# Layer 3's capped mixture: the slot-number products cut in two halves between the fallback's quarters, and every row fetch issued before the first result is sent

## The chip, the cores and the metric

The kernel runs on one core of one Trainium2 chip. The metric is the device time of one execution in microseconds. The whole decoder (four layers, twelve blocks) is one program; the change touches the last block alone, the mixture of experts of layer 3.

## The reference, cut to what matters

The block sees 2048 tokens of 128 features. A router gives each token two of eight experts. Each expert takes its first 320 tokens (CAP); a token that comes later overflows and gets a dense fallback network in place of what it had until then, and is not eligible for later experts.

```python
    def _L3_ffn_ref(x, Wr, W1, b1, W2, b2, fw1, fb1, fw2, fb2):
        D_MODEL, D_FF, N_EXPERTS, TOP_K = (128, 512, 8, 2)
        ...
        CAP = max(int(CAPACITY_FACTOR * (T * TOP_K / N_EXPERTS)), MIN_CAP)
        ...
        y_fb = jax.nn.gelu(xf @ fw1 + fb1, approximate=False) @ fw2 + fb2
        ...
        for e in range(N_EXPERTS):
            assign = experts == e
            w_e = jnp.where(assign, scores, 0.0).sum(-1)
            eligible = assign.any(-1) & ~fb_mask
            rank = jnp.cumsum(eligible.astype(jnp.int32)) - 1
            keep = eligible & (rank < CAP)
            overflow = eligible & ~keep
            fb_mask = fb_mask | overflow
            y = jnp.where(overflow[:, None], y_fb, y)
            idx = jnp.nonzero(keep, size=CAP, fill_value=0)[0]
            valid = jnp.arange(CAP) < keep.sum()
            h = jax.nn.gelu(xf[idx] @ W1[e] + b1[e], approximate=False)
            y_e = h @ W2[e] + b2[e]
            y = y.at[idx].add(y_e * (w_e[idx] * valid)[:, None])
        return y.reshape(Bx, Sx, D)
```

## The kernel before

Each stage of the program gives every engine its own list of instructions, written out by hand; an engine works its list in order, and the lists meet at counting semaphores (`wait_ge`, `then_inc`). There is no scheduler, so the order of the lines is the order on the engine. The stage here is `capped_mixture`. Nearly all its matmuls are recorded under one helper line, L468; the transposes of fetched rows are L3606.

**The dense part.** The fallback runs over all 2048 tokens in four jobs of 512 tokens. A job is an up product (`core.up_pe`, four matmuls of 128x512 into banks 0 to 3), a Gelu on ScalarE (L3421 in the profile, four per job), and a down product (`fallback_down_pe`). The down product of a job is a generator of four quarters. A quarter is four fp32 matmuls of 128x128 and one of a single row for the bias, into bank 6 or 7; ScalarE copies the finished bank away (`lower_act`, L3802).

**The ranks and the slots.** `cap_pe` and `cap_dve` walk the eight experts: VectorE forms who is eligible, two short bf16 products of 16 columns give the ranks, and a fallback quarter of job 0 or 1 stands after each such pair. `places_dve` and `spots_dve` then give each token's two slots: 21 blocks of 128 slots, kept in 32 groups, of which VectorE writes a one-hot `spot` table, four groups to an instruction (L3712, eight instructions), while GpSimd writes the `numbers` table in three instructions (L3831 to L3834). `numbers_pe` multiplies the two: 32 bf16 matmuls of 63 columns, all summed in bank 5, which tell which token fills each slot. `numbers_dve` turns that into two index lists, `source` (L3726) and `target` (L3727). `shares_dve` (seven VectorE instructions, L3731 to L3741) forms the weights with which results are added at the very end.

**The experts.** GpSimd fetches the rows of each expert's tokens out of a table in DRAM by indirect DMA (`fetch_pool`, L3839, one DMA for a block of up to 128 rows, 21 in all; experts 0 to 7 own 3, 2, 3, 2, 3, 2, 3, 3 of them). TensorE transposes them (`slots_pe`, L3606), VectorE copies the result into SBUF (L3761), the up product is four matmuls of 128x320 (`up_pe`), ScalarE's Gelu is L3822, the down product is twelve small matmuls (`down_pe`), and VectorE adds the bias (`result_dve`, L3769 and L3770). TensorE's list is, after the first two experts' slots and the first up product, in rounds: slots of expert n+2, up product of n+1, down product of n. GpSimd then sends each expert's result rows to DRAM, again by indirect DMA (`send_pool`, L3845, 21 in all; 2, 3, 2, 3, 2, 3, 3, 3). SyncE reads the results back (L3882), VectorE adds them to X (L3753), and X is stored (L3885).

**What sets the order around the change.** GpSimd's list is one queue. In it stand the fetches of experts 0 to 3, then a wait for the results of expert 0, its sends, the fetches of expert 4, the sends of expert 1 after a wait, the fetches of expert 5, and so on.

The names of tiles in the profile are those of memory areas: `scratch`, `w_keep` and `w_early` are arenas from which the stage takes its buffers. The fetched rows, their transposes and the results are in `w_keep`, and the weights of this stage in `w_early`.

Of the kernel before, what the change touches and what calls it, by code (L numbers as in the profile page):

```python
# [16 lines left out]
NT = B * HALVES  # L17
# [14 lines left out]
E8 = 8  # L32
# [47 lines left out]
class Signal:  # L80
# [21 lines left out]
    def at(self, *what):  # L102
        return self.of(self.k.stage, *what)
# [74 lines left out]
def tmp(k, cols, dt=F32):  # L178
    return carve(k, "scratch", cols, dt)
# [48 lines left out]
def join(k, e):  # L228

    for last in k.ended:  # L230
        e.wait_ge(*last)


def need(k, e, *packs):

    for name in packs:
        e.wait_ge(k.s.loaded[name].sem, 16)
# [153 lines left out]
def all_flat(k, e, tag):  # L391
    e.wait_ge(*flat(k, tag, 2))
    e.wait_ge(*flat(k, tag, 3))
# [6 lines left out]
def pre_norm_pe(k, pe):  # L400
    turn_pe(k, pe, "pre", lambda i: k.XN[:, i, :], lambda i: normed(k, "pre", i))
# [65 lines left out]
def mm(pe, out, lhsT, rhs, start=True, stop=True):  # L467
    return pe.matmul(out, lhsT, rhs, start=start, stop=stop, skip_group_check=True)  # L468
# [3047 lines left out]
def capped_mixture(k):  # L3516
# [7 lines left out]
    s, w = k.s, k.w  # L3524
# [8 lines left out]
    N2, SB = 2 * NT, SLOT_BLOCKS  # L3533
# [11 lines left out]
    numbers = tmp(k, N2 * 3 * SB, BF16).rearrange("p (i n b) -> p i n b", n=3, b=SB)  # L3545
# [27 lines left out]
    def fallback_down_pe(pe, job):  # L3573
        bank = k.bank[6 + job % 2]
        if job >= 2:
            pe.wait_ge(*s.lowered.at("fallback", job - 2))
        for c in (C - 2, C - 1):
            pe.wait_ge(*s.gated.at("h", job, c))
        for j in range(4):
            o = bank[:, j * P:(j + 1) * P]  # L3580
            for c in range(C):
                mm(pe, o, hidden[job % 2][:, c * BANK + j * P:c * BANK + (j + 1) * P], w["z_fw2"][:, c * D:(c + 1) * D], c == 0, False)
            m = mm(pe, o, w["ones"][0:1, :], w["z_fb2_bc"][0:1, :], False, True)
            if j == 3:
                m.then_inc(*s.summed.up("down", job))
            yield

    def numbers_pe(pe):

        pe.wait_ge(*s.vector.at("rank", E8 - 1))  # L3590
        pe.wait_ge(*s.pool.at("numbers"))
        for i in range(N2):
            if i % 4 == 0:
                pe.wait_ge(*s.cut.at("spot", i // 4))
            m = mm(pe, k.bank[5][:, 0:3 * SB], spot[:, i, :], numbers[:, i, :, :].rearrange("p n b -> p (n b)"), i == 0, i == N2 - 1)
        m.then_inc(*s.projected.up("numbers"))

    def slots_pe(pe, e):
        bank = k.bank[4 + e % 2]
# [27 lines left out]
    def pe(e):  # L3627
        join(k, e)
        need(k, e, "l3f")
        pre_norm_pe(k, e)  # L3630
        all_flat(k, e, "pre")
        core.logits_pe(e)
        core.up_pe(e, 0)
        core.up_pe(e, 1)
        e.wait_ge(*s.preset.at("after"))
        cap_pe(e)
        core.up_pe(e, 2)
        core.up_pe(e, 3)
        numbers_pe(e)
        for job in (2, 3):  # L3640
            for _ in fallback_down_pe(e, job):
                pass
        slots_pe(e, 0)
        slots_pe(e, 1)
        up_pe(e, 0)
        for n in range(E8):
            if n + 2 < E8:
                slots_pe(e, n + 2)
            if n + 1 < E8:
                up_pe(e, n + 1)  # L3650
            down_pe(e, n)
# [48 lines left out]
    def spots_dve(dve):  # L3700

        up, at = lambda n: s.vector.up("spot", n), lambda n: s.vector.at("spot", n)
        dve.wait_ge(*s.vector.at("place", "where"))
        dve.tensor_tensor(reached, where.unsqueeze(2).to_broadcast([P, N2, SB + 1]), starts.unsqueeze(1).to_broadcast([P, N2, SB + 1]),
                          ALU.is_ge).then_inc(*up("reached"))
        dve.wait_ge(*at("reached"))
        dve.tensor_reduce(block_of, reached[:, :, 1:SB + 1], AXX, ALU.add).then_inc(*up("block"))
        dve.wait_ge(*at("block"))
        dve.scalar_tensor_tensor(out=within, in0=block_of, scalar=-float(P), in1=where, op0=ALU.mult, op1=ALU.add).then_inc(*up("within"))
        dve.wait_ge(*at("within"))  # L3710
        for i in range(0, N2, 4):
            dve.tensor_tensor(spot[:, i:i + 4, :], w["steps"][:, 0:P].unsqueeze(1).to_broadcast([P, 4, P]),  # L3712
                              within[:, i:i + 4].unsqueeze(2).to_broadcast([P, 4, P]), ALU.is_equal).then_inc(*s.cut.up("spot", i // 4))

    def numbers_dve(dve):

        up, at = lambda n: s.vector.up("number", n), lambda n: s.vector.at("number", n)
        bank = k.bank[5]
        dve.wait_ge(*s.projected.at("numbers"))
        dve.tensor_scalar(free, bank[:, 2 * SB:3 * SB], -float(OUTSIDE), float(OUTSIDE), ALU.mult, ALU.add).then_inc(*up("free"))  # L3720
        dve.tensor_scalar(later, bank[:, 0:SB], float(NT), -float(T), ALU.is_ge, ALU.mult).then_inc(*up("later"))
        dve.tensor_scalar(number, bank[:, 0:SB], float(P), None, ALU.mult).then_inc(*up("tile"))
        dve.wait_ge(*at("tile"))
        dve.tensor_tensor(number, number, bank[:, SB:2 * SB], ALU.add).then_inc(*up("number"))
        dve.wait_ge(*at("number"))
        dve.tensor_tensor(source, number, later, ALU.add).then_inc(*s.formed.up("source"))  # L3726
        dve.tensor_tensor(target, number, free, ALU.add).then_inc(*s.formed.up("target"))  # L3727

    def shares_dve(dve):
        wgt = core.e3(core.wgt)  # L3730
        dve.tensor_tensor(wgt, wgt, every(live), ALU.mult).then_inc(*s.formed.up("routed"))  # L3731
        dve.wait_ge(*s.formed.at("routed"))
        for n in range(2):
            up, at = lambda x: s.vector.up("share", n, x), lambda x: s.vector.at("share", n, x)
            if n:
                dve.wait_ge(*s.vector.at("share", 0, "sum"))
            dve.tensor_tensor(same, slot, every(place[n]), ALU.is_equal).then_inc(*up("same"))
            dve.wait_ge(*at("same"))
            dve.tensor_tensor(same, same, wgt, ALU.mult).then_inc(*up("own"))
            dve.wait_ge(*at("own"))  # L3740
            dve.tensor_reduce(share[n], same, AXX, ALU.add).then_inc(*up("sum"))  # L3741
# [31 lines left out]
    def dve(e):  # L3773
        join(k, e)
        need(k, e, "l3f")
        pre_norm_dve(k, e)
        for _ in core.route_dve(e, "weights"):
            pass
        e.wait_ge(*s.formed.at("weights"))
        cap_dve(e)  # L3780
        places_dve(e)
        spots_dve(e)
        shares_dve(e)
        numbers_dve(e)
        turned_dve_(e, 0)
        turned_dve_(e, 1)
        for n in range(E8):
            if n + 2 < E8:
                turned_dve_(e, n + 2)
            result_dve(e, n)  # L3790
            if 1 <= n <= QUARTERS:
                fallback_dve(e, n - 1)
        e.wait_ge(*s.vector.at("share", 1, "sum"))
        for n in range(2):
            for q in range(QUARTERS):
                result_sums_dve(e, n, q)
# [39 lines left out]
    def fetch_pool(pool, e):  # L3836
        blocks = fetched_blocks(e)
        for block, n in blocks:
            pool.indirect_dma_start(rows[0:n, block, :], None, row_store, bass.IndirectOffsetOnAxis(ap=source[0:n, block:block + 1], axis=0),  # L3839
                                    bounds_check=T - 1, oob_is_err=False).then_inc(*s.slots_in[e].up(*(("rows",) if block == blocks[-1][0] else ("row", block))))  # L3840
# [7 lines left out]
    def pool(e):  # L3848
        join(k, e)
        e.memset(empty, 0.0).then_inc(*s.preset.up("empty"))  # L3850
        e.tensor_copy(after, w["after"]).then_inc(*s.preset.up("after"))
        for n in range(E8):
            e.memset(first_slot[:, n:n + 1], float(first_slot_of(n) - 1))
        for n in range(SB + 1):
            m = e.memset(starts[:, n:n + 1], float(n * P))
        m.then_inc(*s.pool.up("constants"))
        numbers_pool(e)
        e.wait_ge(*s.rows_out.at("rows"))
        e.wait_ge(*s.formed.at("source"))
        for n in range(4):  # L3860
            fetch_pool(e, n)
        e.wait_ge(*s.emptied.at("results"))
        e.wait_ge(*s.formed.at("target"))
        for n in range(E8):
            send_pool(e, n)
            if n + 4 < E8:
                fetch_pool(e, n + 4)

# [423 lines left out]
```

## Time and profile before

| what | us |
|---|---|
| median of 3 runs | 2503.71 (2494.99 to 2503.94) |
| the profiled execution's own time | 2502.37 |
| its span | 2500.6 |
| the capped mixture, from its first transposes to the end | 2358.1 to 2500.6 |
| TensorE's last matmul begins its group | 2475.53, 5.96 long |

The span is what the profiler saw from the first to the last instruction; the run's own time is 1.77 us longer. Times in rows count from the span's start. "Idle before" in a row's brackets is the time for which that engine did nothing ahead of the group, and the name behind the arrow is what ended it. PEclk is the granted clock of TensorE: 1.00 is 2.4 GHz, 0.50 is 1.2 GHz.

### The profile page before, as it was taken

The numbers are of one execution on the slowest core, as the hardware profiler recorded it, in microseconds if no ns is written. First come the engines' busy times: TensorE is split into PE (matmuls) and PEld (weight loads), VectorE is DVE, ScalarE is ACT, GpSimd is POOL, SyncE is SP. The second block draws the span as 40 slices with busy tenths as digits, with TensorE's granted clock in tenths as the row PEclk, the third lists the DMA queues.
The fourth block names the chain that finished last, engine by engine and source line by source line (L and its number), as shares of the span: only waits on it lengthen the run. The fifth ranks groups of instructions, "written<-read, shape, count | busy, mean of one in ns | idle before, by whom it ended". The sixth has DMA issues, their size and how long they took to land.

```text
span 2500.6 us, 40089 instructions
## 1 busy us (share of the span) xinstructions
PE 2000.8 (80%) x14320; PEld 1350.3 (54%) x14320; DVE 1543.0 (62%) x3580; ACT 1302.8 (52%) x2673; POOL 480.7 (19%) x539
## 2 busy tenths in 40 slices
PE   6999765878999999937764087999999897668795
PEld 4666552436777777613352064565666576434474
DVE  6777685756666566357656925666666457468533
ACT  4666543666777777416654125666666212336521
POOL 2112003103333223241003531000100001211024
PEclk9999986989999999859996598999999899779877
DMA  4000004310000000023201000000000100233102
GB/s 176 1 1 1 1 1 89 85 33 16 1 1 1 1 1 1 1 59 84 45 1 69 0 2 8 1 1 1 1 1 1 46 6 1 99 90 85 52 13 79
DMA packets 78631, 72.35 MB, mean 29 GB/s; under 512 B 8115, under 2 KB 71652, under 8 KB 77410
## 3 DMA queue, kind: packets, MB, share of 16 engines
q1 hardware_dynamic: 77089, 67.29, 9.5%
q0 software_dynamic: 1344, 2.49, 0.4%
q8 instruction: 117, 1.92, 0.3%
q14 instruction: 81, 0.66, 0.1%
HBM read 54.91 MB, written 14.97 MB: 28 GB/s over the span
## 4 chain that ended last, share of the span: by engine, by line
PE 50%; DVE 22%; SPq 9%; issue 7%; ACT 7%; DMA 4%; POOL 1%; DVEq 0%; ACTq 0%; POOLq 0%
PE bank L468 42%; SPq L1408 9%; DMA scratch<-parts 2%; DVE w_keep L1921 1%; PE bank L652 1%; PE bank L2868 1%; PE bank L368 1%; DVE stats L245 1%; PE bank L692 1%; ACT w_early L3109 1%; DVE w_early L2532 1%; DVE scratch L3007 1%; DVE scratch L720 1%; DMA parts<-scratch 1%; DVE XN L3042 1%
## 5 line engine op out<-in xcount | busy, mean ns | idle before, releaser
L468 PE MATMUL bank<-scratch 64*128 64x256 bf16 (+5 forms) x3696 | 397.1, 321 | 127.3 <-DMA scratch<-parts 88.2
L468 PEld LDWEIGHTS bank<-scratch 64*128 64x128 bf16 (+3 forms) x3696 | 222.3, 123 | 274.0 <-issue 80.8
L1225 DVE TENSOR_REDUCE scratch<-bank 128x2 f32<-128x512 f32 x384 | 245.8, 686 | 132.1 <-PE bank L468 129.3
L468 PE MATMUL bank<-w_keep,scratch 128*128 128x128 f32 (+4 forms) x1760 | 247.0, 333 | 35.3 <-ACT scratch L805 20.8
L1311 ACT ACTIVATE w_keep<-bank 128x512 f32<-128x512 f32 x384 | 210.2, 596 | 98.9 <-PE bank L468 93.5
L468 PE MATMUL bank<-XNT,w_keep 128*128 128x256 f32 (+4 forms) x800 | 238.3, 437 | 9.3 <-POOL w_keep L2169 4.6
L468 PEld LDWEIGHTS bank<-w_keep,scratch 128*128 128x128 f32 (+3 forms) x1760 | 184.3, 186 | 97.0 <-issue 46.6
L3109 ACT ACTIVATE w_early<-bank,scratch 128x256 f32<-128x256 f32 x256 | 123.5, 563 | 131.2 <-DVE scratch L3011 131.2
L468 PEld LDWEIGHTS bank<-XNT,w_keep 128*128 128x128 f32 x800 | 149.7, 197 | 62.7 <-issue 29.4
L468 PE MATMUL bank<-w_early,scratch 64*128 64x256 f32 (+3 forms) x1152 | 170.5, 354 | 11.1 <-ACT w_early L3109 8.5
L468 PEld LDWEIGHTS bank<-w_early,scratch 64*128 64x128 f32 (+3 forms) x1152 | 125.2, 192 | 66.3 <-issue 41.2
L468 PE MATMUL bank<-w_keep 128*32 128x256 f32 (+1 forms) x1792 | 136.0, 371 | 8.1 <-ACT w_keep L1311 7.3
L805 ACT ACTIVATE scratch<-bank,scratch 128x256 f32<-128x256 f32 x256 | 100.3, 474 | 77.2 <-DVE scratch L720 77.2
L468 PE MATMUL bank<-scratch,w_early 128*128 128x256 f32 (+2 forms) x416 | 126.0, 448 | 9.9 <-DVE scratch L2527 3.3
L3007 DVE TENSOR_REDUCE scratch<-bank 128x2 f32<-128x512 f32 x128 | 87.9, 686 | 71.4 <-PE bank L468 71.4
L468 PE MATMUL bank<-XNT,w_early 128*128 128x256 f32 (+1 forms) x384 | 119.2, 441 | 4.5 <-ACT XNT L383 1.6
L368 PE MATMUL bank<-w_keep,XN 128*128 128x128 f32 x192 | 47.3, 422 | 84.3 <-DVE XN L318 81.5
L720 DVE TENSOR_REDUCE scratch<-bank 128x2 f32<-128x512 f32 x128 | 82.3, 684 | 50.9 <-PE bank L468 50.8
L468 PEld LDWEIGHTS bank<-w_keep 128*32 128x32 f32 (+1 forms) x1792 | 75.0, 122 | 53.9 <-issue 34.0
L468 PEld LDWEIGHTS bank<-scratch,w_early 128*128 128x128 f32 x416 | 73.4, 203 | 50.1 <-issue 30.0
L1921 DVE SCALAR_TENSOR_TENSOR w_keep<-w_keep,w_early 128x256 f32<-128x256 f32 x192 | 96.5, 551 | 0.1
L468 PE MATMUL bank<-scratch,SEL 64*128 64x512 bf16 x384 | 77.1, 398 | 22.1 <-ACT scratch L1336 22.1
(449 smaller groups left out, 3740.7 us busy)
## 6 DMA issues: line engine op xcount, KB each, us to landing
scratch<-parts SPq DMA_DIRECT2D x768, 32.0 KB
parts<-scratch SPq DMA_DIRECT2D x24, 384.0 KB, 3.2
w_early<-pack_l3f SPq DMA_DIRECT2D x1, 5206.0 KB, 16.0
w_keep<-pack_l2f SPq DMA_DIRECT2D x1, 2124.0 KB, 12.8
w_early<-pack_mamba SPq DMA_DIRECT2D x1, 2120.0 KB, 19.0
w_keep<-pack_l2x SPq DMA_DIRECT2D x1, 2049.0 KB, 7.9
w_keep<-taps SPq DMA_DIRECT2D x4, 512.0 KB, 5.4
w_early<-wave_kernels SPq DMA_DIRECT2D x1, 2048.0 KB
```

Of the source, the lines that this page charges most:

```text
L245: dve.bn_stats(k.stats[:, i, :], src[:, i, :]).then_inc(*k.s.stats.up(tag, i))
L368: t = pe.transpose(k.bank[q][:, j * P:(j + 1) * P], src(i), k.w["ident"])
L468: return pe.matmul(out, lhsT, rhs, start=start, stop=stop, skip_group_check=True)
L652: m = pe.transpose(self.k.bank[3 + o][:, c * S + t * P:c * S + (t + 1) * P], self.expo[g % 4][:, t * S + c * P:t * S + (c + 1) * P], self. ...
L720: dve.tensor_reduce(self.neg[g % 4], self.scores(g)[:, :].rearrange("p (t s) -> p t s", s=S), AXX, ALU.max, negate=True).then_inc(*s.maxed ...
L805: a = act.activation(self.expo[g % 4][:, t * S:(t + 1) * S], self.scores(g)[:, t * S:(t + 1) * S], ACT.Exp, bias=self.neg[g % 4][:, t:t + 1])
L1225: dve.tensor_reduce(neg[:, :, h], self.k.bank[5 - g % 2][:, :].rearrange("p (t s) -> p t s", s=S), AXX, ALU.max, negate=True).then_inc(*s. ...
L1311: act.activation(self.expo[g % 8], k.bank[g % 4][:, :], ACT.Exp, scale=HD ** -0.5).then_inc(*s.weighed.up("e", g))
L1408: sp.dma_start(view[row:row + HD, n, :, :], src).then_inc(*s.loaded_stack(b % 3).up(*((b,) if last else (b, n, o, j))))
L1921: o = dve.scalar_tensor_tensor(out=yv[:, j, :], in0=xv[:, j, tap:tap + S], scalar=scale, in1=yv[:, j, :], op0=ALU.mult, op1=ALU.add)
L3007: dve.tensor_reduce(neg, self.k.bank[o][:, :].rearrange("p (t s) -> p t s", s=S), AXX, ALU.max, negate=True).then_inc(*s.maxed.up("x", p, o))
L3109: a = act.activation(self.expo[(2 * p + o) % 4][:, t * S:(t + 1) * S], self.k.bank[o][:, t * S:(t + 1) * S], ACT.Exp, bias=self.bias[p % 2 ...
```

## The change

Three edits. TensorE's list: the 32 number products are issued in two halves of 16 (`numbers_pe(e, n)`), the first behind the first fallback quarter of job 2 and the second behind the second quarter; before, all 32 stood ahead of job 2. VectorE's list: `numbers_dve` stands ahead of `shares_dve`, no longer behind it. GpSimd's list: all eight experts' fetches stand ahead of all sends.

```diff
-    def numbers_pe(pe):
+    def numbers_pe(pe, n):
 
         pe.wait_ge(*s.vector.at("rank", E8 - 1))
         pe.wait_ge(*s.pool.at("numbers"))
-        for i in range(N2):
+        for i in range(n * NT, (n + 1) * NT):
             if i % 4 == 0:
                 pe.wait_ge(*s.cut.at("spot", i // 4))
             m = mm(pe, k.bank[5][:, 0:3 * SB], spot[:, i, :], numbers[:, i, :, :].rearrange("p n b -> p (n b)"), i == 0, i == N2 - 1)
-        m.then_inc(*s.projected.up("numbers"))
+        m.then_inc(*s.projected.up("numbers", n))
...
         core.up_pe(e, 2)
         core.up_pe(e, 3)
-        numbers_pe(e)
-        for job in (2, 3):
-            for _ in fallback_down_pe(e, job):
+        down = fallback_down_pe(e, 2)
+        for n in range(2):
+            next(down)
+            numbers_pe(e, n)
+        for pieces in (down, fallback_down_pe(e, 3)):
+            for _ in pieces:
                 pass
...
-        dve.wait_ge(*s.projected.at("numbers"))
+        dve.wait_ge(*s.projected.at("numbers", 1))
...
         spots_dve(e)
+        numbers_dve(e)
         shares_dve(e)
-        numbers_dve(e)
...
-        for n in range(4):
+        for n in range(E8):
             fetch_pool(e, n)
         e.wait_ge(*s.emptied.at("results"))
         e.wait_ge(*s.formed.at("target"))
         for n in range(E8):
             send_pool(e, n)
-            if n + 4 < E8:
-                fetch_pool(e, n + 4)
```

On TensorE, behind the up products of jobs 2 and 3 (128x512). The rows 128x63 are number products; a row of four 128x128 and the one under it are one fallback quarter.

```order
 L468 MATMUL bank<-w_early,w_keep 128x128
 L468 MATMUL bank<-XNT,w_early 128x512 x8
-L468 MATMUL bank<-scratch 128x63 x32
 L468 MATMUL bank<-w_early,scratch 128x128 x4
 L468 MATMUL bank<-w_early,w_keep 128x128
+L468 MATMUL bank<-scratch 128x63 x16
 L468 MATMUL bank<-w_early,scratch 128x128 x4
 L468 MATMUL bank<-w_early,w_keep 128x128
+L468 MATMUL bank<-scratch 128x63 x16
 L468 MATMUL bank<-w_early,scratch 128x128 x4
 L468 MATMUL bank<-w_early,w_keep 128x128
```

The products are the same; two quarters of job 2 have moved ahead of the last 16 of them, and one ahead of the first 16.

On GpSimd, before, from the first fetch (`w_keep<-rows`, L3839) to the last send (`results<-w_keep`, L3845):

```order
L3839 DMA w_keep<-rows,scratch 128x128 x10
L3845 DMA results<-w_keep,scratch 4096x128 x2
L3839 DMA w_keep<-rows,scratch 128x128 x3
L3845 DMA results<-w_keep,scratch 4096x128 x3
L3839 DMA w_keep<-rows,scratch 128x128 x2
L3845 DMA results<-w_keep,scratch 4096x128 x2
L3839 DMA w_keep<-rows,scratch 128x128 x2
L3839 DMA w_keep<-rows,scratch 64x128
L3845 DMA results<-w_keep,scratch 4096x128 x3
L3839 DMA w_keep<-rows,scratch 128x128 x2
L3839 DMA w_keep<-rows,scratch 64x128
L3845 DMA results<-w_keep,scratch 4096x128 x11
```

Ten fetches stand ahead of the first send there, and the other eleven behind the sends of experts 0, 1, 2 and 3. The same piece now (the lines are three further on), with the three instructions of the `numbers` table ahead of it:

```order
L3834 TENSOR_TENSOR scratch<-scratch 128x32x21
L3836 TENSOR_TENSOR scratch<-scratch,w_keep 128x32x21
L3837 TENSOR_TENSOR scratch<-scratch,w_keep 128x32x21
L3842 DMA w_keep<-rows,scratch 128x128 x17
L3842 DMA w_keep<-rows,scratch 64x128
L3842 DMA w_keep<-rows,scratch 128x128 x2
L3842 DMA w_keep<-rows,scratch 64x128
L3848 DMA results<-w_keep,scratch 4096x128 x21
```

All 21 fetches have moved ahead of all 21 sends.

## Rows read from the trace of the kernel before

**Rows 1.** Waits from 2396 to 2501: us in total, times, longest.

```profile
POOL results L3845 <- DVE w_keep L3770: 30.5, 6, 17.8
PE bank L3606 <- DMA w_keep<-rows,scratch: 8.1, 2, 4.2
```

**Rows 2.** Timeline of TensorE, number products and fallback: start, us, [idle before].

```profile
2396.41 0.80 PE L468 MATMUL bank<-scratch 128*128 128x63 bf16 x12
2397.51 0.30 PE L468 MATMUL bank<-scratch 128*128 128x63 bf16 x4 [0.30 <-DVE scratch L3712]
...
2399.92 0.39 PE L468 MATMUL bank<-scratch 128*128 128x63 bf16 x4 [0.31 <-DVE scratch L3712]
2400.12 2.06 PE L468 MATMUL bank<-w_early,scratch 128*128 128x128 f32 x8
...
2421.92 1.33 PE L3606 MATMUL bank<-w_keep 128*128 128x128 f32 x5
```

**Rows 3.** Timeline of TensorE, rank products and fallback quarters of jobs 0 and 1.

```profile
2376.96 1.14 PE L468 MATMUL bank<-w_early,scratch 128*128 128x128 f32 x8
...
2378.44 0.18 PE L468 MATMUL bank<-scratch,ONE 128*128 128x16 bf16 x1
```

**Rows 4.** Stretches: us, busy by engine, granted clock (PEclk), DMA share, GB/s.

```profile
2386.00:2388.00 2.00, 2.00 (x18) 1.64 (x18) 0.83 (x6) 0.00 (x0) 0.00 (x0) 1.00 0.05 8
2396.00:2400.00 4.00, 2.38 (x31) 1.28 (x31) 4.00 (x7) 0.95 (x2) 0.31 (x1) 0.96 0.00 0
2400.00:2424.00 24.00, 23.78 (x90) 19.77 (x91) 3.39 (x15) 1.20 (x2) 10.22 (x10) 0.50 0.12 28
2350.00:2355.00 5.00, 2.03 (x13) 1.18 (x11) 1.96 (x7) 1.37 (x2) 0.00 (x0) 1.00 0.00 0
```

**Rows 5.** Timeline of TensorE over the experts' rounds.

```profile
2427.44 0.49 PE L3606 MATMUL bank<-w_keep 128*128 128x128 f32 x3
2432.81 0.44 PE L3606 MATMUL bank<-w_keep 128*128 128x128 f32 x2
2442.36 0.90 PE L3606 MATMUL bank<-w_keep 128*128 128x128 f32 x3 [3.95 <-DMA w_keep<-rows,scratch]
2450.28 0.44 PE L3606 MATMUL bank<-w_keep 128*128 128x128 f32 x2
2460.03 0.64 PE L3606 MATMUL bank<-w_keep 128*128 128x128 f32 x3 [4.16 <-DMA w_keep<-rows,scratch]
2473.37 2.32 PE L468 MATMUL bank<-w_keep,w_early 128*128 128x320 f32 x8
```

**Rows 6.** Timeline of GpSimd: fetches are L3839, sends L3845.

```profile
2403.65 1.25 POOL L3839 DMA_INDIRECT w_keep<-rows,scratch  x1 [7.34 <-DVE scratch L3727]
...
2415.62 0.99 POOL L3839 DMA_INDIRECT w_keep<-rows,scratch  x1 [0.30 <-issue]
2434.43 1.01 POOL L3845 DMA_INDIRECT results<-w_keep,scratch  x1 [17.82 <-DVE w_keep L3770]
2439.74 1.00 POOL L3839 DMA_INDIRECT w_keep<-rows,scratch  x1 [0.30 <-issue]
2479.91 0.98 POOL L3845 DMA_INDIRECT results<-w_keep,scratch  x1 [1.29 <-DVE w_keep L3770]
2486.31 0.92 POOL L3845 DMA_INDIRECT results<-w_keep,scratch  x1 [0.32 <-issue]
```

**Rows 7.** All fetches together, L3839: time from issue to landing.

```profile
DMA to landing us min/median/max: 2.4/2.6/3.6
```

**Rows 8.** Timeline of VectorE: index lists, a fallback sum, the last expert 6 result.

```profile
2401.92 0.17 DVE L3720 TENSOR_SCALAR scratch<-bank 128x21 f32<-128x21 f32 x1
2402.61 0.17 DVE L3727 TENSOR_TENSOR scratch<-scratch 128x21 int32<-128x21 f32 x1
2439.21 1.14 DVE L3746 SCALAR_TENSOR_TENSOR X<-scratch,X 128x128 f32<-128x128 f32 x4
2478.53 0.42 DVE L3769 TENSOR_TENSOR w_keep<-bank,w_early 128x256 f32<-128x256 f32 x1 [4.22 <-PE bank L468]
```

## The prediction, made before the changed kernel was run

> **What bounds the kernel now.** I read the waits of the last hundred microseconds first, then the timelines of TensorE, GpSimd and VectorE there, then the granted clock by stretch. In the waits the reader should see one line that costs time and one that doesn't: TensorE waits 8.1 us for fetched rows, while GpSimd's 30.5 us of waiting for results is the idle time of an engine that waits for work [rows 1]. TensorE's timeline shows a second loss that no wait list has. The number products take from 2396.41 to 2400.12, in which TensorE is busy 2.38 of 4 us, since it takes each group of four as VectorE ends a piece of the spot table [rows 2, 4]. At their end the granted clock falls from 1.00 to 0.50, that is from 2.4 to 1.2 GHz, and stays there for the 24 us that follow, although TensorE is busy in 23.78 of them [rows 4]. So the eight fallback quarters behind them take (2421.92 - 2400.12) / 8 = 2.72 us each [rows 2]; the same quarter took 2376.96 to 2378.44 = 1.48 us at full clock in the ranks stage [rows 3]. In the experts' rounds TensorE stands still for 3.95 and 4.16 us until rows land [rows 5]. Those fetches stand in GpSimd's list behind sends that wait for results: the eleventh isn't issued at about 2417, where the run of ten ends, but only behind the first send at 2434.43 [rows 6]. The results of expert 6 (2478.53) then let the last six sends go, from 2479.91 to 2486.31, and these set the end [rows 6, 8].
>
> **Part 1: number products in halves.** The first quarter starts at 2396.41 where the products did. It waits for Gelus of job 2 and a copied bank that are over by then, since the up products of both jobs are behind it. It takes 1.48, to 2397.89. Sixteen products at 0.80 / 12 = 0.067 take 1.07 [rows 2], to 2398.96; their last piece of the table was there at 2397.51 [rows 2], so there is no gap. The second quarter ends at 2400.44, after the last piece came (2399.92), and the second half at 2401.51. The gaps are gone: 2.14 us in place of 3.71.
>
> The question is the clock. I take it to stay at 1.00. In the ranks stage the same quarters with short bf16 products between them ran at 1.00, and a far thinner stretch, 2350 to 2355 with TensorE busy 2.03 of 5 us, kept it too [rows 4]; what lost it was 3.5 us with nothing but bf16 products of 63 columns and gaps. Now at most 1.07 us of these stand together. Then the six quarters left take 8.88 us and TensorE is through at 2410.4, not 2421.92: 11.5 us. That is 1.6 from the gaps and 8 x 1.24 = 9.9 from the clock. If the clock is lost all the same, from 2401.5, six quarters take 16.3 and 4.1 us are left of the 11.5; if at 2399.9, as before, about 2.5.
>
> The Trainium skill (TensorE: Matmul & The Clock Gate, Part 1: The HAM clock gate) says that a busy array soon gets its full clock back. By that rule the slow stretch would have ended a few quarters in and little would be left to gain here; the trace disagrees, with 0.50 over 2400 to 2424 and 23.78 of 24 us busy [rows 4], so the sum goes by the row.
>
> **Part 2: index lists ahead of the shares.** Before, VectorE ran the seven share instructions and took up the lists at 2401.92; L3727 ended at 2402.78 and the first fetch began at 2403.65 [rows 6, 8]. Now it waits for the products (2401.51, 1.2 us later than the old 2400.31), needs the same 0.86 us from about 2401.6, and the first fetch begins near 2403.3: 0.3 us earlier. The shares come behind, some 2.1 us that end near 2404.6. Their next reader is the last sum, and the next VectorE instruction a copy of transposed rows after 2410: hidden, cost 0. Without the swap the fetches would start some 2 us later.
>
> **Part 3: all fetches first.** Nothing is added: 21 fetches and 21 sends stay. A fetch takes (2415.62 - 2403.65) / 9 = 1.33 us of GpSimd, and lands 2.6 us after issue [rows 6, 7]. Expert 2's third block is the eighth: issued at 2403.3 + 7 x 1.33 = 2412.6, landed at 2415.3. Experts 0 and 1 land at 2408.6 and 2411.2. So TensorE, ready at 2410.4, does the first slots, waits about 0.8 us for expert 1's, runs the first up product (2.3 us, as in [rows 5] at 2473.37) to 2414.1 and waits to 2415.3 for expert 2. This is the row wait that is late next; 2 us, and it eats the time that the clock gave. Expert 2's slots stood at 2427.44 [rows 5]: 12.1 us earlier, in place of 11.5, as the first up product is at full clock too. From there a round takes 5.4 to 5.6 us, and the fetches for one take 2.7 to 4.0, so rows run ahead for good: the last lands at 2403.3 + 20 x 1.33 + 2.6 = 2432.5.
>
> The two stalls go, 3.95 + 4.16. The rounds behind them ran partly at half clock: 2442.36 to 2450.28 is 7.92 against 5.37 for the same shapes from 2427.44 to 2432.81, worth 2.55; 2460.03 to 2473.37 is 13.34 for two rounds against 5.37 + 5.60 [rows 5], from which I leave 0.4 for the third blocks of experts 6 and 7, so 2.0. Together 12.7.
>
> **What stands behind the moved fetches.** The first send goes from 2434.43 to 2403.3 + 21 x 1.33 = 2431.2, so even it is earlier, though expert 0's result waits for it from 2421. Nothing waits for that send: results have a buffer of their own for every block. What counts is the sixteenth send, expert 6's first. GpSimd reaches it at 2431.2 + 15 x (2486.31 - 2479.91) / 5 = 2450.4 [rows 6]; expert 6's result is ready at 2478.53 - 24.8 = 2453.7 and its send 1.4 later [rows 6, 8]. GpSimd has 4.7 us of slack and the tail behind it is as before.
>
> The Trainium skill (SBUF - State Buffer, SBUF: two separate sides) warns that a DMA issued from GpSimd starves for descriptors while VectorE runs a two-port instruction, and gives 620 ns growing to about 3100. The shares now run beside the first fetch or two. By that rule all fetches slip by up to 2.1 us, TensorE waits as much longer for expert 2, and the gain would be 22.7. The trace doesn't bear it out: beside VectorE's fp32 sum at 2439.21 to 2440.35 the fetch at 2439.74 took 1.00 us, as others did [rows 6, 8].
>
> **Sum.** 12.1 up to expert 2's slots and 12.7 behind: 24.8 us. The profiled execution took 2502.37, so 2477.6, rounded to 2478. Its time is 1.3 us under the median shown (2503.71), and one of the three runs took 2494.99 without a change, so some 9 us can come from elsewhere in the program.
>
> **Rivals.** A: the clock falls at the number products anyway. For it speaks that bf16 products still fill 2.1 of 5.1 us and that it takes long to return; against it the stretch in [rows 4] that was thinner and kept it. Fetching is untouched, so 2.5 to 4.1 + 0.6 + 12.7 = 15.8 to 17.4 us are gained, and less if the clock is also slow in the first rounds (by about 2.5): 2485 to 2489, say 2487.
>
> B, the other side: GpSimd becomes the bound, since 42 indirect DMAs stand in one run. Fetches may slow once more than ten are issued on end, of which no row tells, and every send is behind them. The end is then 2403.3 + 41 steps. At 1.33 nothing is lost; over (2461.5 - 2403.3) / 41 = 1.42 us a step the gain shrinks, at 1.7 it is half gone (2490), and from 2.02 the kernel is slower than before; at 2.4, 2519. Against it: ten fetches kept 1.33 with a landing time of 2.6 [rows 6, 7], so two or three are under way whatever stands behind, and DMA share is 0.12 [rows 4].
>
> C: the new order doesn't remove the stalls because the landing, not the queue, is what TensorE waits for. With landing at 2.6 to 3.6 us [rows 7] against the 17 us for which the eleventh fetch was held back, this could leave 1 us a round at most: 2483.
>
> **Numbers.** Forecast 0.80, A 0.09, B 0.06 (half of it slower than before), C 0.05. The forecast's own range is 2474 to 2482. The range has to take in the 9 us between runs on the low side and A on the high side: 2468 to 2489. A measurement of this kernel tells 0.5% (12.5 us) from no change; the forecast, C and nearly all of A are beyond it: faster 0.91, same 0.06, slower 0.03.
>
> **What would show it.** In the profile after: PEclk at 1.00 from 2390 to 2420; fallback quarters of 1.48; the slots of expert 0 at 2410 to 2411; two short row waits before 2416 and none behind; 21 fetches from 2403.3 to 2431 at 1.33; up products of 2.3 in all rounds; the last six sends without a gap near 2455 to 2461. It is wrong if the clock row near 2401 says 0.50, if the fetch steps grow, or if VectorE's result of expert 6 is over a microsecond old when its send begins because GpSimd is still busy.

## The result, and the profile after

| | median us | lowest to highest |
|---|---|---|
| before, 4 runs | 2501.81 | 2494.99 to 2503.94 |
| changed, 4 runs | 2472.35 | 2461.48 to 2477.20 |

The ratio is 0.9881 with a 95% interval of 0.984 to 0.9921. The medians are 29.5 us apart, where 24.8 were forecast. The profiled execution took 2461.48 us (span 2459.7), 40.9 less than the profiled one before. That difference is two things. The stage's first transposes say where the block begins:

```profile
L368 PE MATMUL bank<-w_keep,XN x16: 278/421/474, 2343.6 to 2347.3; 128*128 128x128 f32 x16
```

It began at 2358.1 before, so 14.5 us were gained ahead of everything that the change touches. I therefore measure **the block alone**, from there to the end of the span: 142.5 us before, 116.1 after, 26.4 us less.

TensorE in the changed kernel, from the number products on (start, us, [idle before]); it answers to [rows 2, 5]:

```profile
2382.99 0.68 PE L468 MATMUL bank<-scratch 128*128 128x63 bf16 x16
2383.51 1.14 PE L468 MATMUL bank<-w_early,scratch 128*128 128x128 f32 x8
...
2384.99 0.68 PE L468 MATMUL bank<-scratch 128*128 128x63 bf16 x16
2385.50 1.13 PE L468 MATMUL bank<-w_early,scratch 128*128 128x128 f32 x8
...
2394.49 0.55 PE L3606 MATMUL bank<-w_keep 128*128 128x128 f32 x3
2395.59 0.44 PE L3606 MATMUL bank<-w_keep 128*128 128x128 f32 x2 [0.55 <-DMA w_keep<-rows,scratch]
...
2399.44 0.55 PE L3606 MATMUL bank<-w_keep 128*128 128x128 f32 x3 [1.26 <-DMA w_keep<-rows,scratch]
...
2404.87 0.44 PE L3606 MATMUL bank<-w_keep 128*128 128x128 f32 x2
...
2410.30 0.49 PE L3606 MATMUL bank<-w_keep 128*128 128x128 f32 x3
```

The two halves of the products run without a gap, the six quarters behind them take (2394.49 - 2385.50) / 6 = 1.50 us each, and the only row waits are the two short ones. The stretches, to be read beside [rows 4], with the granted clock third from the end:

```profile
2381.00:2385.50 4.50, 4.50 (x54) 3.62 (x53) 4.21 (x6) 1.31 (x2) 0.66 (x1) 1.00 0.00 0
2385.50:2409.50 24.00, 22.19 (x141) 17.53 (x138) 5.22 (x19) 7.52 (x14) 17.18 (x17) 1.00 0.18 44
```

GpSimd, beside [rows 6]: the first and last fetch, the first send, and the send groups of experts 5 and 6.

```profile
2387.44 1.25 POOL L3842 DMA_INDIRECT w_keep<-rows,scratch  x1 [5.78 <-DVE scratch L3734]
...
2413.67 0.95 POOL L3842 DMA_INDIRECT w_keep<-rows,scratch  x1 [0.30 <-issue]
2414.92 1.03 POOL L3848 DMA_INDIRECT results<-w_keep,scratch  x1 [0.30 <-issue]
...
2434.32 0.98 POOL L3848 DMA_INDIRECT results<-w_keep,scratch  x1 [3.62 <-DVE w_keep L3773]
...
2439.16 0.98 POOL L3848 DMA_INDIRECT results<-w_keep,scratch  x1 [1.29 <-DVE w_keep L3773]
```

GpSimd is idle ahead of both groups, so it waits for results and not the other way round. In this profile every step that was forecast is there; two sizes are off, and they are taken up behind the experiments.

### The profile page after: what moved, and what is told of

Same layout as the page of the kernel before. It is cut to its first block, busy times and chain, and to the rows that moved or that the text cites. A ratio compares the mean times of both kernels' runs of the same rounds, so it can differ in the third digit from the quotient of the medians.

```text
span 2459.7 us, 40090 instructions
## 1 busy us (share of the span) xinstructions
PE 1973.1 (80%) x14320; PEld 1335.8 (54%) x14320; DVE 1543.7 (63%) x3580; ACT 1302.7 (53%) x2673; POOL 480.2 (20%) x539
## 4 chain that ended last, share of the span: by engine, by line
PE 51%; DVE 23%; SPq 8%; issue 7%; ACT 7%; DMA 3%; POOL 1%; DVEq 0%; ACTq 0%; POOLq 0%
PE bank L468 43%; SPq L1408 8%; DMA scratch<-parts 2%; DVE w_keep L1921 1%; PE bank L652 1%; PE bank L2868 1%; PE bank L368 1%; DVE stats L245 1%; DVE scratch L1225 1%; PE bank L692 1%; ACT w_early L3109 1%; DVE w_early L2532 1%; DVE scratch L3007 1%; DVE scratch L720 1%; DVE XN L3042 1%
## 5 line engine op out<-in xcount | busy, mean ns | idle before, releaser
L468 PE MATMUL bank<-w_early,scratch 64*128 64x256 f32 (+3 forms) x1152 | 162.5, 345 | 11.1 <-ACT w_early L3109 8.5
L468 PEld LDWEIGHTS bank<-w_early,scratch 64*128 64x128 f32 (+3 forms) x1152 | 118.2, 183 | 65.2 <-issue 39.2
L3193 POOL TENSOR_TENSOR w_early<-XN 128x1024 f32<-128x1024 f32 x16 | 30.3, 1892 | 331.4 <-ACT XN L3142 331.4
```

The lines of the kernel that those rows point to most:

```text
L3193: pool.tensor_tensor(self.ksquares[t], self.raw[t], self.raw[t], ALU.mult).then_inc(*s.pool.up("squares", b, t))
```

## The experiments

Twelve runs followed, four on each of three chips: e1 to e4, e5 to e8, e9 to e12. The table is made from their profiles, one for each. e4 to e7 have no other execution, so for them the block alone counts. "Run" is the longest row of indirect DMAs that GpSimd issues without a break of over 0.7 us, at about 1.3 us a step where nothing else is said; "slow stretch" is explained at the third kernel.

| kernel | block begins | block us | run | slow stretch |
|---|---|---|---|---|
| before | 2358.1 | 142.5 | 11 | no |
| changed | 2343.6 | 116.1 | 33 | no |
| e1 halves, old fetch order | 2359.6 | 127.9 | 11 | no |
| e2 fetches ahead, products in one piece | 2363.6 | 136.5 | 21 | yes |
| e3 changed, again | 2359.6 | 127.7 | 21 | yes |
| e4 products together behind two quarters | 2365.2 | 127.5 | 21 | yes |
| e5 before, again | 2356.0 | 141.8 | 11 | no |
| e6 products behind one quarter | 2354.5 | 127.7 | 21 | yes |
| e7 shares first | 2359.5 | 127.2 | 21 | yes |
| e8 up product first | 2358.6 | 127.2 | 21 | yes |
| e9 fetch steps of 2.0 | 2361.7 | 124.1 | 13 | yes, in the sends |
| e10 fetch steps of 2.5 | 2351.1 | 130.6 | 16 | yes, in the sends |
| e11 thirteen fetches ahead | 2359.1 | 122.3 | 13 | short ones |
| e12 changed, third time | 2363.8 | 128.0 | 21 | yes |

**e1: number products and index lists as changed, fetches as before.**

```diff
-        for n in range(E8):
+        for n in range(4):
             fetch_pool(e, n)
...
             send_pool(e, n)
+            if n + 4 < E8:
+                fetch_pool(e, n + 4)
```

> The number products in halves and the index lists ahead of the shares, with the fetches left behind the sends as before. I measure the block alone: from its first transposes (L368) to the end of the span, 142.5 us before and 116.1 after. Theory (two separate losses that add): the clock stays at 1.00 over the fallback and expert 0's down product is through 13.4 us earlier, but the two stalls of 3.95 and 4.16 us for rows and the half clock behind them stay; block 129 us. Rival (a faster fallback only makes TensorE wait longer for the held fetches): the stalls grow, block 135 us or more. Rival (the clock falls all the same without the changed fetches): fallback quarters of 2.7 us, block about 141.

2488.5 us, ratio 0.9917 (0.9892 to 0.9943); block 127.9, that is 14.6 less than before, where 13.4 were expected. TensorE in it:

```profile
2423.30 3.07 PE L468 MATMUL bank<-w_early,scratch 128*64 128x128 f32 x24
2430.26 0.55 PE L3606 MATMUL bank<-w_keep 128*128 128x128 f32 x3 [3.88 <-DMA w_keep<-rows,scratch]
...
2447.14 0.98 PE L3606 MATMUL bank<-w_keep 128*128 128x128 f32 x3 [4.18 <-DMA w_keep<-rows,scratch]
```

The clock was kept (1.00 from 2395 to 2420) and both stalls stayed at their old length (3.95 and 4.16 in [rows 5]). The two losses are separate; both rivals fall.

**e2: all fetches ahead, products as before.** The change's last edit alone.

> All 21 fetches ahead of the sends, with the number products in one piece ahead of the fallback as before. Theory: the clock falls at 0.50 where it did, the eight quarters take 2.7 us each and no row wait is left at all, because TensorE is late; both stalls go and the rounds run at full clock; block 142.5 - 13 = 129.5 us, so that this and the other half alone add to the whole 26.4. Rival (GpSimd's run of 42 becomes the bound or the stalls have another cause): block over 133.

2505.1 us, ratio 0.9979 (0.9958 to 1.0); block 136.5, not 129.5. That is past the 133 of the rival, but by neither cause that it names: GpSimd still waits for results ahead of its sends, and the stalls did come from the order of the fetches. The fallback was at 1.2 GHz as expected and the stalls for rows were gone, but one of another kind stood in the first up product, first TensorE and then VectorE:

```profile
2427.33 1.33 PE L3606 MATMUL bank<-w_keep 128*128 128x128 f32 x5
2436.16 3.84 PE L468 MATMUL bank<-w_keep,w_early 128*128 128x320 f32 x8 [7.50 <-issue]
```

```profile
2435.55 0.56 DVE L3761 COPY w_keep<-bank 128x384 f32<-128x384 f32 x1 [27.35 <-remote]
```

The transposes ended at 2428.66 and VectorE's copy of them came at 2435.55, released by nothing that the profile knows ("remote"). Taking off those 7.5 us leaves 129.0 (an estimate), where the theory had 129.5.

**e3: the changed kernel again.**

> The changed kernel as it is, a second profile. In the first profile the block begins 14.5 us earlier than before (2343.6 against 2358.1), though nothing ahead of it changed. Theory (that is the spread of the rest of the program between runs, from stretches of half clock that fall differently): the block is 116.1 +- 0.7 again, and its start lies elsewhere, between 2343 and 2362. Rival (the new program is laid out differently and runs faster ahead of the block): it starts at 2343 to 2346 again, in this and in every kernel with the change.

2490.4 us, ratio 0.9922 (0.9905 to 0.9939). The block began at 2359.6, and that of the unchanged kernel (e5, below, on another chip) at 2356.0: the 14.5 us gained ahead of the block in the first profile were spread of the rest of the program. But the block was 127.7 us, outside what I expected. TensorE, between the slots of expert 3 and those of expert 4:

```profile
2420.73 0.44 PE L3606 MATMUL bank<-w_keep 128*128 128x128 f32 x2
2421.00 0.43 PE L468 MATMUL bank<-w_keep,w_early 128*128 128x320 f32 x1
2422.05 0.43 PE L468 MATMUL bank<-w_keep,w_early 128*128 128x320 f32 x1 [0.61 <-issue]
...
2424.19 0.52 PE L468 MATMUL bank<-w_keep,w_early 128*128 128x320 f32 x1 [0.72 <-issue]
...
2429.16 0.59 PE L468 MATMUL bank<-w_early,scratch 128*64 128x128 f32 x2 [1.41 <-issue]
2430.59 0.37 PE L468 MATMUL bank<-w_early,scratch 128*64 128x128 f32 x1 [0.84 <-issue]
2431.99 1.10 PE L468 MATMUL bank<-w_early,scratch 128*64 128x128 f32 x3 [1.03 <-issue]
...
2437.61 0.84 PE L3606 MATMUL bank<-w_keep 128*128 128x128 f32 x3
```

This is the **slow stretch**: for some 12 us TensorE takes one or two instructions every 0.7 or 1.4 us, with gaps inside one row of matmuls where no wait stands. The round takes 16.88 us against 5.43 above, 11.45 more, which is nearly the whole 11.6 by which the block is longer. It isn't TensorE's alone: VectorE and ScalarE have waits by "remote" of up to 15.20 and 8.9 us there. Expert 0's down product ended at 2420.79 and VectorE added its bias at 2433.56, 12.8 us later. GpSimd's fetches keep their step, and TensorE's last gap ends at 2433.42, 2.8 us after the last fetch is issued:

```profile
2429.69 0.95 POOL L3842 DMA_INDIRECT w_keep<-rows,scratch  x1 [0.30 <-issue]
2435.08 1.03 POOL L3848 DMA_INDIRECT results<-w_keep,scratch  x1 [4.44 <-DVE w_keep L3773]
```

Two causes can be read off as absent. From 2421 to 2434 the DMA engines carried GpSimd's own transfers and nothing else, so no loading of instructions, which the profile lists as a queue of its own, stood in the way:

```profile
DMA packets 286, 0.52 MB, mean 40 GB/s; under 512 B 144, under 2 KB 144, under 8 KB 286
## 3 DMA queue, kind: packets, MB, share of 16 engines
q0 software_dynamic: 286, 0.52, 13.3%
```

Nor were these transfers slow: by the packets' own times, those of the fetches issued in the stretch were over 2.0 to 2.4 us after the start of their issue, and those of the same fetches in the first profile 2.2 to 2.8.

**e4: all 32 number products together, behind two quarters.**

```diff
         for n in range(2):
             next(down)
+        for n in range(2):
             numbers_pe(e, n)
```

> All 32 number products in one piece, but behind two fallback quarters. Theory (the clock was lost because TensorE waited for the spot table, and two quarters are as long as the table takes): the 32 run without a gap in about 1.1 us, the clock stays at 1.00, block 116.1 +- 0.7. Rival (bf16 products of 63 columns lose the clock when many stand together, and the halves are what saves it): clock 0.50 behind them, six quarters at 2.7 us, block about 121 to 122 (7.4 more, less the 1.8 us of row waits that they fill).

Block 127.5 with a slow stretch, so it is read against e3 (127.7), not against 116.1. The products, and the stretch that holds them and the fallback:

```profile
2406.24 1.18 PE L468 MATMUL bank<-scratch 128*128 128x63 bf16 x32
```

```profile
2403.00:2416.00 13.00, 13.00 (x113) 10.95 (x112) 6.71 (x19) 1.66 (x3) 5.68 (x7) 1.00 0.09 21
```

The 32 products took 1.02 us, to 2407.26, and the clock held at 1.00. So halving them isn't needed to keep it; that two quarters stand ahead of them is enough.

**e5: the kernel before again.**

> The kernel before as it is, a second profile. Theory (spread of the rest of the program): the block is 142.5 +- 1.5 us long again and begins anywhere between 2343 and 2362. Rival (the changed program's front part is faster): it begins at 2358 +- 2.

Begin 2356.0, block 141.8 as expected, stalls of 3.88 and 4.17, no slow stretch. Its begin, 2 us from the first one, would fit the rival too; the begins of e3, e12 and the other kernels that hold the change (2351.1 to 2365.2) are what rules it out.

**e6: all 32 behind one quarter.** In e4's edit, `next(down)` once.

> The changed kernel, with all 32 number products behind the first quarter of job 2 only. The products then begin some 2.2 us before the spot table is done, so half of them run with gaps; the thin stretch is 2 us in place of the 3.5 us before. Theory (it takes a thin stretch as long as the old one): clock stays at 1.00, block 116.1 +- 0.7. Rival (any gaps among the bf16 products lose it): clock 0.50 behind them, seven quarters at 2.7, block about 123 to 124.

Block 127.7 with a slow stretch. Twelve of the 32 products came with gaps of 0.23 to 0.30 us, and still:

```profile
2393.81 0.85 PE L468 MATMUL bank<-scratch 128*128 128x63 bf16 x20
2394.89 0.30 PE L468 MATMUL bank<-scratch 128*128 128x63 bf16 x4 [0.23 <-DVE scratch L3715]
...
2396.10 0.30 PE L468 MATMUL bank<-scratch 128*128 128x63 bf16 x4 [0.30 <-DVE scratch L3715]
2396.23 1.14 PE L468 MATMUL bank<-w_early,scratch 128*128 128x128 f32 x8
```

```profile
2392.00:2406.00 14.00, 13.16 (x111) 10.87 (x110) 6.78 (x19) 1.73 (x3) 6.74 (x7) 1.00 0.10 25
```

So gaps among these products don't lose the clock by themselves. Of the cause I can say that the products spread over 3.7 us lost it (in before, e2 and e5, each time 0.50 behind them) and spread over 2.4 us here didn't. What lies between the two, and which property of the stretch counts, isn't shown.

**e7: shares ahead of the index lists**, with the products as changed.

> The changed kernel with the seven share instructions ahead of the index lists again. Theory: VectorE takes up the lists 1.7 us later, every fetch goes 1.7 us later, and since TensorE waits for expert 2's rows, the block grows by all of it: 117.8 us, waits of about 2.2 and 1.3 us in place of 0.55 and 1.26. Rival (that wait is not on the path): 116.1.

Block 127.2 with a slow stretch, so its length settles nothing. The way there does: expert 2's slots came 57.3 us into the block (2416.81) against 55.7 in e3 (2415.29), 1.6 us later as expected; TensorE's one row wait, 1.95 us, was for expert 1's rows.

```profile
2413.05 0.44 PE L3606 MATMUL bank<-w_keep 128*128 128x128 f32 x2 [1.95 <-DMA w_keep<-rows,scratch]
```

**e8: expert 1's up product ahead of expert 2's slots.** In `pe`, `up_pe(e, 1)` moved ahead of `slots_pe(e, 2)`.

> The changed kernel with expert 1's up product ahead of expert 2's slots on TensorE, so that it fills the 1.26 us wait for expert 2's rows. Theory: the wait goes and the block is 115.0 +- 0.3 us, 1.1 less. Rival (the Gelus of expert 0 or the copied slots are late next): 116 or more. In time against the kernel before the ratio should be that of the change, a whisker lower, 0.986 to 0.989.

2489.5 us, ratio 0.995 (0.9933 to 0.9968), not the 0.986 to 0.989 expected. The wait for expert 2's rows was gone (only 0.6 us for expert 1's was left), but the slow stretch stood in the rounds behind and the block was 127.2, within 0.5 us of e3. Inconclusive on the 1.1 us.

**e9 and e10: the fetches of experts 3 to 7 slowed.** One fill of GpSimd with a wait for it ahead of each of them, or three:

```diff
         for block, n in blocks:
+            for turn in range(3 if e >= 3 else 0):
+                pool.memset(empty, 0.0).then_inc(*s.pool.up("pause", block, turn))
+                pool.wait_ge(*s.pool.at("pause", block, turn))
             pool.indirect_dma_start(rows[0:n, block, :], None, row_store, ...
...
+        e.wait_ge(*s.emptied.at("results"))
         for n in range(E8):
             fetch_pool(e, n)
-        e.wait_ge(*s.emptied.at("results"))
```

(A wait that stood between the fetches and the sends had to go ahead of the fetches as well; the first one still began 43.7 and 43.8 us into the block, as in e3.)

> The changed kernel, in which each fetch from expert 3's on is preceded by one small fill on GpSimd and a wait for it, so that 13 of the 21 steps grow from 1.30 to some 1.5 to 1.6 us. Five profiles with all fetches ahead show, from about 15 us into the run of fetches to 3.5 us behind its last, a stretch in which TensorE, ScalarE and VectorE take one instruction every 0.7 us or so (waits by issue or remote), worth 11.5 us; the first profile and the kernels that fetch ten at a time don't. Theory (the unbroken pace of indirect DMAs is what slows the other engines' instructions): a slower pace shortens the slow stretch, block 117 to 124 us. Rival (it has nothing to do with GpSimd's pace): block 127.5 +- 1 as in the five.

> The same with three fills and waits before each fetch from expert 3's on, steps of 2.0 us or more. Theory: no slow stretch at all, no issue wait of TensorE over 0.3 us behind the first slots. The fetches end some 10 us later, and the sixteenth send is late by 4 to 7 us, so the block is 120 to 123 us. Rival (the pace has no part in it): the slow stretch of 11.5 us is there and the block over 128.

A fill with its wait costs more than I took: steps of 2.0 and 2.5 us. e9: 2488.8 us, ratio 0.9936 (0.9916 to 0.9957), block 124.1, 0.1 past the theory's range. e10: 2495.5, 0.9956 (0.9938 to 0.9974), block 130.6, not 120 to 123 and past the rival's 128. In both, the rounds beside the fetches have no slow stretch; in e10 TensorE waited 1.54 and 1.88 us there for rows that now came late. The slow stretch comes later, when GpSimd works off the sends at 1.3 us a step; e10's run of 16 is its last fetch and 15 sends. e9's GpSimd, last paced fetch and the sends behind it:

```profile
2441.17 0.95 POOL L3845 DMA_INDIRECT w_keep<-rows,scratch  x1 [0.77 <-POOL scratch L3843]
2442.43 1.03 POOL L3851 DMA_INDIRECT results<-w_keep,scratch  x1 [0.30 <-issue]
...
2456.65 0.98 POOL L3851 DMA_INDIRECT results<-w_keep,scratch  x1 [0.30 <-issue]
2461.39 0.98 POOL L3851 DMA_INDIRECT results<-w_keep,scratch  x1 [3.75 <-DVE w_keep L3773]
```

and its TensorE, in the last down products:

```profile
2454.83 0.49 PE L468 MATMUL bank<-w_early,scratch 128*128 128x128 f32 x3 [1.14 <-issue]
...
2459.78 6.53 PE L468 MATMUL bank<-w_early,scratch 128*128 128x128 f32 x34 [0.33 <-issue]
```

It moved with the unbroken run of DMAs, from the fetches to the sends, which the rival can't explain. That "no slow stretch at all" would follow was wrong for e10: I had slowed the fetches and not thought of the sends.

**e11: thirteen fetches ahead, the rest one expert deeper than before.**

```diff
-        for n in range(E8):
+        for n in range(5):
             fetch_pool(e, n)
...
+            if n + 5 < E8:
+                fetch_pool(e, n + 5)
```

> The changed kernel with the fetches of experts 0 to 4 ahead (13) and each later expert's behind a send, as in the kernel before but one expert deeper. Theory: the run of fetches ends at 17 us and with it the slow stretch, which costs 0 to 3 us; the rows of expert 6 come behind two experts' sends and cost TensorE a wait of 2 to 4 us; block 118 to 122, the shortest in the chip's time. Rival (depth is what counts, the slow stretch comes from elsewhere): block 127 or more.

2488.9 us, ratio 0.9937 (0.9911 to 0.9964); block 122.3. That is 0.3 past the theory's range and well under the rival's 127. The issue gaps of TensorE sum to 1.7 us and none is over 0.54, but ScalarE and VectorE had "remote" waits of 9.5 and 7.8 us while GpSimd issued 20 DMAs with breaks of 1.6 and 2.6 us. The wait for expert 6's rows, expected at 2 to 4 us, didn't show.

**e12: the changed kernel on the chip of e9 to e11.**

> The changed kernel as it is, on the chip of the three others. If the slow stretch belongs to the change and the first profile was the exception, the block is 127.5 +- 1 again; if it comes and goes between executions, 116.

2492.8 us, ratio 0.9954 (0.9934 to 0.9973), block 128.0. Its waits from 2420 to 2440, where GpSimd ends its run of 21 at 2435.1:

```profile
DVE w_keep L3772 <- remote: 14.4, 1, 14.4
ACT scratch L3825 <- remote: 14.4, 4, 7.4
PEld bank L468 <- issue: 9.7, 11, 1.9
PE bank L468 <- issue: 5.9, 9, 1.0
```

So of the changed kernel's three profiles two have the slow stretch, as have the variants that keep its run of fetches; the first profile is the exception.

## Why the prediction was right, and where it wasn't

The median, 2472.35, lay in the range; the forecast's own range (2474 to 2482) missed it by 2 us. The first profile bears out the sum of Parts 1 to 3: 26.4 us in the block against 24.8. Part of the hit is luck all the same: the medians of the repeats on other chips, e3 and e12, lie 20.9 and 12.7 us under those of the kernel before, and by the second of these the time would have been at the range's upper edge.

**The clock (Part 1)** was kept, shown in the changed kernel and by e1, e4 and e6; fallback quarters 1.50 us for the forecast 1.48. The credit went to the wrong word, though: it isn't the halves that keep it (e4).

**The number products** were mis-sized. I read 0.067 us each from a row of twelve, 1.07 a half; a half took 2383.51 - 2382.99 = 0.52. TensorE reached the slots 50.9 us into the block and not 52.3. VectorE had the products' sums as much earlier, so the first fetch began 43.8 us into the block and not 45.2, and expert 2's slots, which wait for it, 55.8 and not 57.2. This 1.4 us is most of the 1.6 that the sum lacked.

**Index lists (Part 2).** The first fetch came 1.7 us earlier than before (43.8 us into the block against 45.6), not 0.3, by the same mis-sized products. Without the swap TensorE is 1.6 us late at expert 2's slots (e7). The shares ran on VectorE beside the first two fetches, and these took 1.25 and 1.00 us, the first as much as alone in [rows 6]: they weren't slowed. The row that the prediction held against such a cost (VectorE's fp32 sum beside one fetch) was thinner evidence, since nothing shows that sum to be a two-port instruction.

**The stalls (Part 3)** went, and the wait that took their place was named: 0.55 and 1.26 us for the rows of experts 1 and 2 against 0.8 and 1.2. The fetches stepped at 1.31, the first send came 27.5 us behind the first fetch (27.9 forecast), and GpSimd had its slack at expert 6's send.

**The sum's two halves** are separate: e1 alone gives 14.6 us, and e2 alone 6.0, or 13.5 with its 7.5 of slow stretch taken off. That makes 28.1 against 26.4 for both, so they add only roughly: e2, at half clock, is too late to wait for rows, which costs the changed kernel 1.8.

**What failed** is in rival B. I excluded a cost of the long run because ten fetches kept their step and landing time, and looked for the cost on GpSimd's own step. The step did stay near 1.3 throughout 21 and 33 DMAs. The cost came on the other engines: 11.5 us in e3. The moved fetches, worth 11.8 us between e1's block and that of the first profile (127.9 and 116.1), were worth 0.2 between e1's and e3's (127.9 and 127.7). In the timed runs of that chip e1 (fetches as before) and e3 (all ahead) are the same too, 0.9917 and 0.9922. So where the slow stretch occurs, the edit of the fetches is worth next to nothing and the change is worth what its first part gives. The size of the gain therefore depends on the occasion: 0.9881 in the first measurement, 0.9922 (0.9905 to 0.9939) and 0.9954 (0.9934 to 0.9973) in the later ones.

**What stays open.** In the profiles of the three chips a slow stretch stands where GpSimd issues 13 or more indirect DMAs at 1.3 us a step (in e11, with milder signs, 13, 10, 5 and 5 with breaks of 1.6 to 3.6 us between them), and in none with runs of 11 or fewer, nor in 13 fetches at 2.0 or 2.5. But the first profile has a run of 33 without one. What differs there is the record of GpSimd's DMAs. The first two profiles have every landing:

```profile
DMA to landing us min/median/max: 2.5/2.6/3.6
```

Each of the 42 DMAs raises its semaphore 16 times as it lands, and the traces of before and of the first changed profile hold all 672 of these updates. The twelve later traces hold 257 to 400, so most fetches have no landing time in them, in e5 as in e3. Records missing is not enough for a slow stretch: e1 and e5 have 318 and 400 and none. But the slower pace eases both together: e10's fetches at steps of 2.5 us have 195 of their 208 updates, e9's at 2.0 have 129, and neither has a slow stretch beside them, while e3's fetches at 1.3 have 73 of 336. So a plausible suspect, argued and not shown, is that whatever records the semaphores fills up over a long unbroken row of DMAs and holds up the engines. The chip may differ as well, and no run settles it. All executions here are recorded by the profiler, so whether the stretch exists without it is open too, and with it whether the unrecorded gain is nearer to 26 or to 15 us. And by what rule the clock falls was not tried further.

None of the other versions is shown to be faster than the changed kernel: e9 and e11 were on the same chip as e12, their blocks are 3.9 and 5.7 us shorter, but the intervals of their timed ratios overlap its own.

## What to carry to other kernels

A low clock behind a thin stretch can cost more than the stretch itself (here 8 x (2.72 - 1.50) = 9.8 us against 3.7 - 1.0 = 2.7); filling the wait for a slow producer with dense work that is ready cured both here. When a queue's work is pulled ahead, check what the longer unbroken run does to the other engines, not only its own step: look for "issue" gaps inside rows of matmuls and for "remote" waits. And when a change sits in one block of a long program, measure that block in the profile, since its begin moved by 22 us between runs, and take a second profile before believing the first.

## What the runs showed of the hardware that was not expected

While GpSimd issued 13 to 21 indirect DMAs at 1.3 us a step, TensorE, VectorE and ScalarE were held up together in ten of the eleven profiles with such a run (mildly in e11). In e3 TensorE got through one or two instructions per 0.7 or 1.4 us, and in no profile did the stretch last more than 3.1 us beyond the end of the last DMA's issue. It moved with the run when the run was moved (e9, e10). Whether it is there without the profiler is open. Number products that stood ready took 0.033 us each (0.52 for 16), half of what their row in a gappy stretch ([rows 2], 0.80 for 12) suggested.
